# Where the norms, a transpose, the slot writes and two subtractions stand in a one-core decoder layer

## The reference

```python
x = x + attn(layernorm(x), Wq, Wkv, Wo, bo)      # 16 heads of 32, 4 key heads, ALiBi, mask
x = x + xattn(layernorm(x), ctx_512, ctx_512)    # 32 heads of 16, 8 key heads, 256 context rows
x = x + ffn(layernorm(x), gate_w, ...)           # 32 experts, top 4 of 2 groups, and a shared expert
...
cw = sigmoid(sum(abs(x), axis=-1))               # a weight for each token, in attn
q = (x * cw) @ Wq;  kv = x @ Wkv
...
oh = one_hot(topk_idx);  pos = cumsum(oh) - 1    # slot of a token in its expert, 128 slots each
out = scatter(experts(gather(x))) + (silu(x @ shared_gate) * (x @ shared_up)) @ shared_down
```

## Time and profile before

| | us |
|---|---|
| median of three runs | 1081.57 |
| the profiled execution, its own time | 1084.14 |
| its span | 1082.3 |
| stages 3 to 6, each | 88.1, 88.9, 90.3, 86.7 |
| PE busy in the span | 927.7 |
| DVE busy in the span | 572.7 |
| mean granted TensorE clock | 0.929 |

### The profile page before, as it was taken

The page is one execution under the profiler, slowest core; times in us unless marked ns, Lnnn a source line. Parts: engine busy times, 40 slices in busy tenths (PEclk is TensorE's granted clock), DMA queues, the critical chain, the costliest instruction groups (busy, mean ns, idle before and its releaser), DMA issues.

```text
span 1082.3 us, 16193 instructions
## 1 busy us (share of the span) xinstructions
PE 927.7 (86%) x6123; PEld 565.7 (52%) x6168; DVE 572.7 (53%) x1300; ACT 349.3 (32%) x699; POOL 303.6 (28%) x306
## 2 busy tenths in 40 slices
PE   5376899889988989898998898987999899988990
PEld 4335535645754754674574475463577455534540
DVE  2334945857757756784785785784342122212220
ACT  4020064255246326316424523524410122211120
POOL 4001000110240240142024024014215054565674
PEclk9578589899999999998999999998999999999895
DMA  4902202302300400330240230071233499989643
GB/s 135 315 2 78 59 3 67 91 3 65 93 23 23 128 10 2 95 102 2 67 111 23 61 97 3 5 266 63 87 148 89 162 322 320 328 263 308 142 62 35
DMA packets 73248, 115.14 MB, mean 106 GB/s; under 512 B 12482, under 2 KB 47584, under 8 KB 73168
## 3 DMA queue, kind: packets, MB, share of 16 engines
q1 hardware_dynamic: 55236, 94.42, 26.9%
q0 software_dynamic: 14480, 16.55, 8.1%
q10 hardware_dynamic: 3456, 3.15, 1.0%
HBM read 70.90 MB, written 16.88 MB: 81 GB/s over the span
## 4 chain that ended last, share of the span: by engine, by line
PE 56%; DVE 20%; DMA 7%; issue 6%; ACT 4%; POOL 3%; SPq 2%; another core or an unknown queue 1%; POOLq 0%; DVEq 0%; ACTq 0%
PE qa L1620 7%; DVE mxx L1027 5%; PE qa L1285 4%; DMA out<-arena,half_ids 4%; PE qx L1371 4%; PE pt L1203 4%; PE qa L1203 4%; PE qx L1607 4%; PE qa L1489 4%; ACT arena L628 3%; PE qx L1427 3%; PE vb L1438 3%; SPq L364 2%; PE qa L1456 2%; PE qa L1319 2%
## 5 line engine op out<-in xcount | busy, mean ns | idle before, releaser
L628 ACT ACTIVATE arena<-qx 128x512 f32<-128x512 f32 x256 | 148.7, 601 | 160.4 <-PE qx L1427 131.6
L1027 DVE TENSOR_REDUCE mxx<-qx 128x2 f32<-128x512 f32 x256 | 168.2, 685 | 36.5 <-PE qx L1371 34.7
L490 POOL TENSOR_TENSOR rstd<-mv,power 128x2 f32<-128x2 f32 x24 | 16.8, 701 | 449.1 <-DVE mv L855 449.1
L628 ACT ACTIVATE arena<-qa 128x512 f32<-128x512 f32 (+2 forms) x125 | 67.4, 540 | 209.7 <-PE qa L1620 100.8
L1427 PE MATMUL qx<-arena 98*128 98x512 bf16 x256 | 97.4, 404 | 34.5 <-ACT arena L628 23.0
L1620 PE MATMUL qa<-arena 128*128 128x512 f32 x256 | 117.6, 603 | 1.1 <-ACT arena L628 1.1
L1371 PE MATMUL qx<-arena 96*128 96x256 bf16 x512 | 103.3, 291 | 16.4 <-DVE mxx L1027 14.7
L1074 DVE RECIPROCAL rd<-va 128x192 f32<-128x192 f32 x32 | 43.5, 1358 | 95.4 <-PE va L1484 95.4
L1438 PE MATMUL vb<-arena 128*32 128x256 f32 x1024 | 85.6, 407 | 1.2 <-ACT arena L628 0.2
L615 POOL DMA_INDIRECT out<-arena,half_ids x44 | 68.6, 1558 | 62.9 <-DMA out<-arena,half_ids 29.0
L1371 PEld LDWEIGHTS qx<-arena 96*128 96x128 bf16 x512 | 45.9, 102 | 61.8 <-DVE mxx L1027 33.6
(11 more groups left out here) (201 smaller groups left out, 1563.7 us busy)
## 6 DMA issues: line engine op xcount, KB each, us to landing
arena<-in_L_ffn_w SPq DMA_DIRECT2D x96, 512.0 KB
qs<-arena SPq DMA_DIRECT2D x24, 384.0 KB, 5.0
arena<-arena SPq DMA_DIRECT2D x72, 128.0 KB, 2.4
res<-in_x SPq DMA_DIRECT2D x8, 512.0 KB, 8.0
xnd<-arena SPq DMA_DIRECT2D x8, 512.0 KB
ks<-arena SPq DMA_DIRECT2D x48, 64.0 KB, 2.0
arena<-arena SPq DMA_DIRECT2D x48, 64.0 KB, 2.0
arena<-arena ACTq DMA_DIRECT2D x24, 128.0 KB, 3.1
```

The lines of the kernel that those rows point to most:

```text
L628: nc.scalar.activation(dst, src, func, **kw).then_inc(s[signal], 1)
L1027: v_.reduce_max(mxx[:, col:col + 3:2], xbank[v % 2].rearrange("p (h n) -> p h n", h=2), AX.X).then_inc(s["x_max"], 1)
```

## The change

`AT_SELF` moves the self-attention scores one to two steps earlier (first at v = 15, last at 26), `AT_ROWS` goes from 29 to 28. `AT_SLOTS` goes from 23 to 15, so that the slot writes stand behind the second piece in POOL's order and ahead of the third. `AT_NORM` goes from 25 to 27 and `AT_FIRST` from 28 to 25, so the next sequence's transposes come first, and they wait for the second norm's statistics. The first norm and the sums on ACT go from cross steps 15, 16, 18 to 18, 19, 20. Both low-part subtractions go from DVE to POOL. `token_weights` goes on DVE from behind `cross_out(1)` to directly behind the second norm. The held eighths of the shared expert are issued ahead of the cross step instead of behind it, and the wait for the evicted piece goes from `self_scores(0)` to `self_scores(1)`.

```diff
-        AT_SELF = (17, 18, 19, 21, 22, 24, 25, 27)
-        AT_HALF, AT_ROWS, AT_SLOTS = 17, 29, 23
+        AT_SELF = (15, 17, 18, 20, 21, 23, 24, 26)
+        AT_HALF, AT_ROWS, AT_SLOTS = 17, 28, 15
-        AT_OUT, AT_NORM, AT_FIRST = 20, 25, 28
+        AT_OUT, AT_NORM, AT_FIRST = 20, 27, 25
...
+                if a:
+                    pool.wait_ge(s["q_hi"], k + 1)
+                    nc.gpsimd.tensor_tensor(ql, qf, qh.bitcast(F32), ALU.subtract).then_inc(s["q_split"], 1)
                 for v in range(XU):
+                    if a and v == AT_CONTEXT + 6:
+                        pool.wait_ge(s["c_mid"], k + 1)
+                        nc.gpsimd.tensor_tensor(kp[2], kr, kp[1], ALU.subtract).then_inc(s["c_split"], 1)
...
-                        if n and v == 15:
+                        if n and v == 18:
                             norm_apply(1, k + 1, xn1)
-                        if n and v == 16:
+                        if n and v == 19:
                             token_sums(k + 1, 0)
                             token_sums(k + 1, 1)
-                        if n and v == 18:
+                        if n and v == 20:
                             token_sums(k + 1, 2)
...
-                def queries_low():
-                    dve.wait_ge(s["q_hi"], k + 1)
-                    v_.tensor_tensor(ql, qf, qh.bitcast(F32), ALU.subtract).then_inc(s["q_split"], 1)
...
-                def context_low():
-                    dve.wait_ge(s["c_mid"], k + 1)
-                    v_.tensor_tensor(kp[2], kr, kp[1], ALU.subtract).then_inc(s["c_split"], 1)
...
                     norm_apply(2, k, xn2)
+                    if n:
+                        token_weights(k + 1)
...
                     cross_out(1)
-                if n:
-                    token_weights(k + 1)
...
-                        if k in FIRST_PIECE and k > 2:
-                            wait_evicted(pe, FIRST_PIECE[k] + 1)
+                    if u == 1 and k in FIRST_PIECE and k > 2:
+                        wait_evicted(pe, FIRST_PIECE[k] + 1)
...
                     for v in range(LEAD):
+                        for n_ in HELD[v] if v < len(HELD) else ():
+                            shared_slot(n_)
                         if v < 2:
                             pe.wait_ge(s["x_max"], k * XU - 1 + v)
                         cross(v)
-                        for n_ in HELD[v] if v < len(HELD) else ():
-                            shared_slot(n_)
...
                             pe.wait_ge(s["xn1"], k + 2)
+                            pe.wait_ge(s["ln2_stats"], k + 1)
                             transpose_norm(xn1, qa, "x_t")
```

More of the change, by code:

```diff
@@ L1031, in _ @@
                                 queries()
-                            elif v == AT_QUERY[3] + 3:
-                                queries_low()
                             elif v == AT_CONTEXT + 3:
                                 context_rem()
-                            elif v == AT_CONTEXT + 6:
-                                context_low()
                             if v in AT_SELF:
```

## The result

The changed kernel took 1106.76 us (median of four runs: 1102.07, 1102.53, 1110.99, 1111.19), the kernel before it 1082.46 beside it on the same chip: ratio 1.0224, 95% interval [1.0178, 1.0269], slower by 24.3 us where +7.8 was forecast. Only the direction held; the time lies 10.8 us beyond the range's end.

A forecast was written before the change was run, and what follows sets the result against it. PE's order was taken as the bound, so longer stages lengthen the whole. Terms summed to +7.8 on the profiled 1084.14, giving 1091.9, or 1089.4 as a median; range 1070 to 1096.

The forecast's parts named there:

- What bounds it: Whole kernel: PE's order is the path, stages 3 to 6 repeat, at most 8.7 us idle per stage.
- Slot writes, stages 3 to 7: Late signals move with the writes into the score section and cost about the same: 0, bounds -16.4 and +5.
- Rival C: Lateness costs more in PE and DVE's ping-pong, +1 in each of five stages, with PE's clock falling: 1094, chance 0.14.
- Stage 8: Shifted steps: POOL comes 10 us sooner, 6.8 can go, late signal takes perhaps 4: -2.9, bounds -6.8 and 0.
- Tail: New PE waits of 1.84 and 1.8 for cross_out: +1.66 each in stages 1 to 6, +2.3 in stage 7.
- Stage 0 to 1: Earlier token weights cut PE's wait of 3.66: -2.5; slower subtraction +0.5; together -2.0.
- Scores and subtractions: Score section: PE waits 1.4 us for query DMAs delayed by the POOL subtraction, balance +0.97 per stage.
- Norm and sums: Projections: PE's 0.90 wait at step 18 behind ACT's norm goes, -0.90 in stages 1 to 6.
- Held eighths: First shifted step: they fill the 1.14 wait but put off the first exponential, 0, bounds -0.9 and +0.4.

The follow-up runs named there:

- e6: The changed kernel with the slot writes put back at v = 23: 1094.11 us, ratio 1.0126 to the kernel before.
- e1: The kernel before with only the slot writes moved behind v = 15: 1081.32 us, ratio 0.9989.
- e2: The kernel before with only the tail's edit, reordered transposes and token weights right behind the second norm: 1098.99 us, ratio 1.0159.
- e17: The kernel before with only the token weights right behind the second norm in every stage, transposes in old order: 1079.17 us, ratio 0.9965.
- e3: The kernel before with only the self scores from v = 15 and both subtractions on GpSimd: 1082.11 us, ratio 1.0013.
- e7: The changed kernel with the self scores and both subtractions put back as before: 1092.78 us, ratio 1.0118 to the kernel before.
- e13: The changed kernel with four slot writes behind v = 15 and four behind v = 23: 1084.03 us, ratio 1.0026 to the kernel before.
- e11: The kernel before with four slot writes behind v = 15 and four behind v = 23: 1056.98 us, ratio 0.9807.

## Why the prediction was wrong

**What bounds it** was right: PE's order, and stages that repeat. The error lies in what a wait costs.

**Slot writes, stages 3 to 7: the step that failed first.** It said that the lateness "costs there about what it costs here", 0 with bounds -16.4 and +5, and with stage 8 -2.9. Alone that is near the truth (-17.2 and +22.0: +4.8 by the windows, just inside, and -1.2 in the total). In the changed kernel the same edit costs 10.6 us (e6), 13.5 more than the sum had. Against e6 the score sections are 28.9 us longer (205.2 against 176.3), at a granted clock of 0.88 to 0.92 where e6 has 1.00. The shifted steps are only 5.5 shorter, because the other edits had already brought them from 127.6 to 109.5. That makes +23 by the windows, 19 more than alone: 12 for the gain that was already drawn, 7 for dearer score sections. About half comes back later: from stage 8's first shifted step on, the changed kernel takes 331.99 us at a clock of 0.96, e6 343.44 at 0.94. The sum priced the writes against the kernel before, where the shifted steps' idle time was still to be had. Rival C named the mechanism of the dearer part, the ping-pong and the falling clock, at +1 a stage; by the windows it is +4.7 a stage, and the gain already drawn stood in no rival.

**Stage 8: right for this edit alone.** Windows of its first shifted steps, the kernel before and e1, over nearly the same instructions:

```profile
736.41:756.76 20.35, 16.17 (x96) 7.20 (x98) 7.40 (x37) 9.92 (x21) 9.23 (x11) 0.83 0.02 2
```

```profile
745.91:760.60 14.69, 14.41 (x99) 7.46 (x97) 7.36 (x34) 9.84 (x21) 4.10 (x6) 0.97 0.01 2
```

-5.7 there and +2.8 in the score section ahead (30.89 instead of 28.12) are the -2.9 of the sum. In the changed kernel it was more, -6.2 (13.89 instead of 20.35, and 28.38 ahead of it), with the held eighths' move in it.

**Tail: the waits right, the clock left out.** +1.66 a stage was said. By the windows a tail is 2.0 longer at full clock (2.0 to 2.2 in the changed kernel). Where the clock fell, in five tails of six in e2 and three of six in the changed kernel, 0.6 to 1.7 come on top: 16.9 us over six in e2, where 10.0 stood in the sum. With stages 0 and 7 the sum had +9.8 for this edit; e2 measured +17.2. Rows 6 in the kernel before had shown it: behind its wait of 4.11 PE ran at half speed. The prediction used that for stage 8 and for nothing of its own new waits of 1.8 us. Stage 0 to 1 was right at its wait:

```profile
94.10 0.68 PE L1230 MATMUL qa<-arena,ones 128*128 128x128 f32 x4 [1.21 <-ACT arena L634]
```

(1.2 said, 3.66 in the earlier trace rows), but the gain there is larger than the 2.5 of the sum: 3.8 in e17.

**Scores and subtractions: the term right, its balance wrong.** +0.97 a stage, measured 1.1 (e3); what the shifted steps give back, 1.3 a stage, stood nowhere. In all the term was +6.3 (five stages, two halves and stage 0); alone it measured +1.4, in the changed kernel 11.5 (e7). The subtraction at 1.81 us and the wait of 1.4 were right. The Trainium skill (Perfetto Trace Analysis, Optimizing Scalar/DVE Operations) warned that such a move might not help, for a shared port. Together with the scores' move it gained nothing (ratio 1.0013); no run moves the subtractions alone. The reason that the page gives doesn't show: DVE's reduction takes 688 ns on average in stage 4 of the changed kernel, 685 in the kernel before.

**Norm and sums:** -5.4 said, -6.8 measured alone. **Held eighths:** 0 said with a bound of -0.9 a stage, -7.2 alone: they fill the 1.14 us of the earlier trace rows, and 0.9 us of PE's work a stage no longer stands in the shifted steps. In the full sum neither gain could be added to the others, for the floor.

**Adding up.** The five parts alone give -1.2 + 17.2 + 1.4 - 6.8 - 7.2 = +3.4, the whole +24.2. So 21 us lie between the parts and the whole: by the table, about 11 in the score sections and 12 in the shifted steps. The four parts other than the slot writes show it. Together they cost 13.6 us with the writes at v = 23 (e6 against before), 25.4 with them at v = 15 (the changed kernel against e1) and 23.7 with them split (e13 against e11). With the writes at 23 these parts take 18.1 us out of the shifted steps; in the other two cases the writes' lateness is gone from there and they find only 6.1 to 6.4. Adding terms that were each priced against the kernel before was the method's own fault, more than any single term. That the forecast had the sign right says little for it: its tail term was too small, and its terms for the slot writes and the held eighths missed in opposite directions.

**Still open:** why PE's signals come late in the second half and at the end of a row of indirect DMAs, why eight cost and six don't, what makes the score sections longer than their parts even without the row of eight in them (e6, e13), and why the changed kernel's four runs lie at two levels 9 us apart. No run takes the DMAs out and keeps GpSimd busy, so whether it is the DMAs or GpSimd's time wasn't told apart.

## What to carry to other kernels

Price a new wait of PE in a tight section with the clock behind it: here a wait of 1.8 us cost 0.6 to 1.7 us more in the tails where the clock fell, eight of twelve. Price an edit in the kernel that the other edits leave, not in the one before: gains that fill the same idle time are drawn once, losses are paid each time, so look for the floor of a section (PE busy) before adding them. Before an edit that repairs the changed kernel is taken for the cause, try it on the kernel before: here the split gained the same in both. A row of eight DMA issues on one queue that delays others may be worth cutting in two before it is worth moving.

## What the runs showed that was not expected

Eight indirect DMAs in a row on GpSimd (1.27 us apart) go with DVE and ACT starting up to 3.8 us late on PE's results. Cutting the row into four and four gained 21 us of 1081, in the kernel before and in the changed one alike. Where the row stands alone decides little: 1081.3 (v = 15), 1080 to 1084 (v = 23) and 1078.4 us (ahead of all).
